# Pairwise interaction tower on one core: look-ups spaced by GpSimd's own memsets in place of waits for TensorE

## The reference

```python
e = jnp.stack([tbl_0[ids[:, 0]], ..., tbl_31[ids[:, 31]]], axis=1)      # 1024 x 32 x 64
p, q = e[:, ROW], e[:, COL]                                             # 496 pairs
kp = jnp.einsum('bpj,ipj->bpi', p, kernel)
z = jnp.sum(kp * q, axis=-1)                                            # 1024 x 496
h = jnp.concatenate([z, dense_ctx], axis=1)
h = jnp.maximum(h @ W_top1 + b_top1, 0.0)                               # 512
h = jnp.maximum(h @ W_top2 + b_top2, 0.0)                               # 256
y = h @ W_top3                                                          # 1
```

## Time and profile before

| | |
|---|---|
| time, three runs | 498.26 us median, 494.0 to 500.97 |
| span of the profiled execution | 412.5 us |
| that execution's time outside its span | not recorded; the median of the runs is 85.8 us above the span |
| TensorE busy | 403.7 us, 98% |
| VectorE busy | 298.6 us, 72% |
| ScalarE busy | 259.1 us, 63% |
| GpSimd busy | 231.6 us, 56% |
| look-ups (indirect DMAs) | 244, 945 ns each on GpSimd |
| TensorE's granted clock, mean | 0.996 |

### The profile page before, as it was taken

How to read it: one execution, slowest core, us unless ns; L and a number is a source line. 1 busy time by engine, 2 the same in 40 slices (tenths; PEclk the granted TensorE clock), 3 DMA queues, 4 the chain that set the end, 5 groups by cost and what they waited for, 6 DMA issues and landing times.

```text
span 412.5 us, 10180 instructions
## 1 busy us (share of the span) xinstructions
PE 403.7 (98%) x3421; PEld 254.4 (62%) x3421; DVE 298.6 (72%) x293; ACT 259.1 (63%) x1874; POOL 231.6 (56%) x251
## 2 busy tenths in 40 slices
PE   7889999999999999999999999999999999999997
PEld 5556656667675766666766665666666566654442
DVE  6776887878788887878979798878879888740000
ACT  6476877667577876764796867719978667002221
POOL 6777777777677757776766777677767200000000
PEclk9998999999999999999999999999999999999999
DMA  6665661131281111211211113111311020000000
GB/s 177 210 200 155 191 221 33 27 77 27 37 219 28 29 19 47 61 28 25 63 42 28 25 25 79 24 27 26 79 25 27 15 51 2 2 2 0 2 0 1
DMA packets 18266, 24.31 MB, mean 59 GB/s; under 512 B 6387, under 2 KB 11767, under 8 KB 17958
## 3 DMA queue, kind: packets, MB, share of 16 engines
q1 hardware_dynamic: 10406, 15.64, 13.0%
q0 software_dynamic: 7808, 8.01, 9.7%
HBM read 19.44 MB, written 0.00 MB: 47 GB/s over the span
## 4 chain that ended last, share of the span: by engine, by line
PE 92%; DMA 3%; POOL 3%; issue 1%; ACT 0%
PE u_ps L690 41%; PE z_ps L724 14%; PE u_ps L711 13%; PE z_ps L730 7%; PE u_ps L771 7%; PE t_ps L644 4%; PE u_ps L791 3%; POOL nat L419 3%; DMA nat<-tbl,ids_sb 2%; PE u_ps L697 2%; DMA ids_sb<-ids 1%; PE t_ps L677 0%; PE u_ps L799 0%; ACT y_sb L571 0%
## 5 line engine op out<-in xcount | busy, mean ns | idle before, releaser
L419 POOL DMA_INDIRECT nat<-tbl,ids_sb x244 | 230.5, 945 | 90.7 <-issue 56.6
L607 DVE TENSOR_TENSOR prod<-u_ps,rows 128x1024 f32<-128x1024 f32 x184 | 213.5, 1218 | 56.7 <-PE u_ps L690 56.7
L504 ACT ACTIVATE pass_prod<-pass_prod 128x64 f32<-128x64 f32 x896 | 214.3, 243 | 22.1 <-DVE pass_prod L618 22.1
L690 PE MATMUL u_ps<-rows,k_sb 64*128 64x256 f32 x1472 | 176.2, 387 | 0.0
L504 ACT ACTIVATION_READ_ACCUMULATOR pass_prod<-pass_prod 128x1 f32 x896 | 169.9, 190 | 0.0
L690 PEld LDWEIGHTS u_ps<-rows,k_sb 64*128 64x128 f32 x1472 | 139.0, 188 | 46.0 <-DVE pass_prod L618 13.4
L618 DVE TENSOR_TENSOR pass_prod<-u_ps,nat 128x1024 f32<-128x1024 f32 x56 | 67.2, 1215 | 1.2 <-PE u_ps L711 1.2
L711 PE MATMUL u_ps<-k_sb,rows 64*128 64x256 f32 x448 | 61.5, 394 | 0.6 <-ACT rows L492 0.6
L724 PE MATMUL z_ps<-prod,sel 128*32 128x512 f32 x512 | 61.6, 598 | 0.0
L492 ACT ACTIVATE rows<-t_ps 128x512 f32<-128x512 f32 (+1 forms) x38 | 19.6, 516 | 54.2 <-PE t_ps L644 54.0
L711 PEld LDWEIGHTS u_ps<-k_sb,rows 64*128 64x128 f32 x448 | 40.6, 186 | 14.6 <-DVE prod L607 9.6
(11 more groups left out here) (50 smaller groups left out, 78.9 us busy)
## 6 DMA issues: line engine op xcount, KB each, us to landing
by_self<-rows SPq DMA_DIRECT2D x32, 128.0 KB
nat<-tbl,ids_sb POOLq DMA_INDIRECT x244
k_sb<-kern SPq DMA_DIRECT2D x3, 768.0 KB, 5.6
k_sb<-kern SPq DMA_DIRECT2D x2, 640.0 KB, 5.7
k_sb<-kern SPq DMA_DIRECT2D x1, 1152.0 KB, 5.2
k_sb<-kern SPq DMA_DIRECT2D x2, 512.0 KB
rows<-w SPq DMA_DIRECT2D x1, 1024.0 KB, 6.6
rows<-tbl SPq DMA_DIRECT2D x4, 224.0 KB
```

The lines of the kernel that those rows point to most:

```text
L419: pool.indirect_dma_start(nat_of(m, n)[:, h * EMBED:(h + 1) * EMBED], None, tables[f], bass.IndirectOffsetOnAxis(ids_sb[:, col:col + 1], 0 ...
L504: op = nc.scalar.activation(of, of, ACT.Copy, accum_out=z_nat[:, b % 2, s, row:row + 1])
L607: nc.vector.tensor_tensor(to, u, by.unsqueeze(1).to_broadcast([P, 2, 2, SIZE]), ALU.mult).then_inc(prod_ready, 1)
L690: op = nc.tensor.matmul(u[:, h, :], k_sb[part, k_of(d), side, :], rows[part, tile, cols_of(b)], start=True, stop=True)
```

## The change

From m = SPACED = 12 on, the two waits ahead of a look-up are left out. In their place GpSimd writes zeros to a tensor `zeros` of 128x128 f32 that nobody reads, and waits for the semaphore of this write, with a count that is higher by one each time; then it issues the look-up. The waits of tiles m < 12, the ring's wait and the wait ahead of tile 0 stay, and so do the order and all work of the other engines.

```diff
+SPACED = 12
...
+        zeros = sb("zeros", [P, P])
...
+        zeros_there = sem("zeros_there")
...
                 for n in range(SUBS):
                     for h in range(2):
-                        _, pieces, quads = PLAN.in_front(m, 2 * n + h)
-                        if pieces:
-                            pool.wait_ge(u_ready, pieces)
-                        if quads:
-                            pool.wait_ge(summed, quads)
+                        if m < SPACED:
+                            _, pieces, quads = PLAN.in_front(m, 2 * n + h)
+                            if pieces:
+                                pool.wait_ge(u_ready, pieces)
+                            if quads:
+                                pool.wait_ge(summed, quads)
+                        else:
+                            nc.gpsimd.memset(zeros[:], 0.0).then_inc(zeros_there, 1)
+                            pool.wait_ge(zeros_there, 4 * (m - SPACED) + 2 * n + h + 1)
                         f = 2 * tile + h
                         col = (b * SUBS + n) * FIELDS + f
                         pool.indirect_dma_start(
```

## The result

The changed kernel takes 594.13 us (median of four runs, 592.71 to 596.87), the kernel before beside it 497.08 us (494.0 to 500.97). The ratio is 1.197, with a 95% interval of [1.1917, 1.2023]. I had forecast 546 us: the sign is right, but the cost is 97 us and not 48.

A forecast was written before the change was run, and what follows sets the result against it. TensorE was taken to bound the kernel, with GpSimd's look-ups hidden; steps of 1.58 us would delay it 47.5 us, so 412.5 + 47.5 = 460, plus 85.8 gives 546 us; range 509 to 598 us.

The forecast's parts named there:

- The sum by late look-ups: TensorE's transposes wait for later look-ups: 47.5 us at pair 58/59, span 412.5 to 460, time 546 us.
- L: The prediction's theory: look-ups come later and TensorE waits for them, delay D = 192p - 255.9 for a step p.
- The step of 1.58 us: GpSimd, look-up start to start from tile 12 on: 0.94 + 0.20 + 0.20 + 0.24 us, ends 1.44 and 1.72.
- the memset must sit out: GpSimd, between a look-up's reported end and the memset's start: 0.20 us taken, between 0.12 and 0.30.
- Rival B: On GpSimd the memset starts at the look-up's reported end: step 1.38 us, delay 9.1, time 507 us; chance 0.12.
- The 2.2 us of landing: Time from a look-up's start until its data has landed, taken alike for all pairs, about 2.2 us.
- Rival D: All 1.25 us of a look-up lie ahead of the memset: step 1.69, 567 us; 0.2 within the forecast's 0.66.
- I leave the 85.8 as it is: The runs' median 498.26 us lies 85.8 above the profiled span; this was added unchanged to the span of 460.
- Nothing on TensorE's path goes with them: gain at the end, nothing: Removing the waits ahead of 208 look-ups, 15 us in all with the ring's, was priced at nothing.
- Last start near 376: Sign on GpSimd: the last look-up would start near 376 us, where the profile before had 322.22.
- Clock: TensorE's low clock, 1.7 us of work per wait, would only eat waiting; after the last wait +1.7 us could show.
- rival C: Changing between memset and look-up makes look-ups last 1.27 us: 628 us, milder forms 573 to 598; chance 0.12 together.

The follow-up runs named there:

- both: The kernel before with its waits kept and the memsets with their waits added from tile 12 on; 439.04 us on chip 7, ratio 1.0629.
- before_third: The kernel before, unchanged, run once more for its profile; 491.17 us beside 492.59, ratio 1.0007.
- waits_off_again: The kernel before with the two waits left out from tile 12 on and no memset in their place; 635.69 us beside 492.59, ratio 1.2973.
- after_again: The changed kernel, unchanged, run again; 577.8 us (564.16 to 578.72), the kernel before beside it 491.12.
- cols360: The changed kernel with a memset of 360 two-byte columns in place of 128 f32 columns; 493.34 us beside 492.59, ratio 1.0046.

## Why the prediction was wrong

**The sum by late look-ups: near on a 412 chip, and worth nothing in the runs that I forecast.** On chip 7 the memsets cost 26.7 us, L with the measured step 21 to 23.5. In the changed kernel all look-ups landed 40 us and more ahead of their transposes, so the 48 us of the forecast aren't among the 97. That the sign came out right is luck. The changed kernel itself never ran on a 412 chip; 433 to 439 us there is my estimate from L and `both`.

**The step of 1.58 us: too large by 0.14.** The term was the 0.20 us that "the memset must sit out". It is 0.00. The 0.30 us between two look-ups belong to the next one's start and not to the last one's end; my split of 0.12 to the end rested on look-ups that wait for other engines. The memset's 0.22 and the round trip's 0.27 were near what I took (0.20, 0.24). Rival B's reasoning was right and its 1.38 too low by these. The 2.2 us of landing were 2.44 at pair 58/59, and 5 beside the load of the weights. Rival D, and with it the rule of the Trainium skill that the instruction goes on past its reported end (Perfetto Trace Analysis, "DMA Instruction — SWDGE (GPSIMD)"), doesn't show here: GpSimd did its memset from that end on.

**"I leave the 85.8 as it is": wrong, and the first failed step.** I took the difference of the runs' median and one execution's span for time outside the span. Time outside is 1.8 us. The 85.8 us lie inside the span, in executions of a kind that the profile didn't show, in which TensorE is held up (`before_third`: span 489.1 us), and such time isn't left as it is by a change to the look-ups.

**"Nothing on TensorE's path goes with them: gain at the end, nothing": wrong, and the step that cost most.** It was true for the profile that I read and false for the runs that I forecast. On 490 chips taking the waits out costs 143 us (waits_off_again), with a memset of 0.22 us in their place still 87 to 97 by the medians (73 in the fastest run of after_again). I had bounded the removal below by nothing without a reason that excludes a loss: I asked who waits for GpSimd, not what its pauses are worth to the others.

**The signs that I named.** Look-ups 1.58 us apart: 1.44. Last start near 376: 472.5. Transposes that wait for look-ups, 18 times and 48 us together: none among the 24 pairs, instead GpSimd waits 106.2 us for the transposes. TensorE's share down to 88%: 81%. Clock: a mean of 0.874, below full in all windows with look-ups; I had hidden it in waits for look-ups, and it did lie beside waits, of another kind. That 594 falls into my range of 509 to 598 is luck: its upper end was rival C's, whose mechanism (look-ups as slow as the first, 1.27 us) isn't there: they last 0.95.

**What stays open.** What makes one chip a 490 chip; and what it is inside such a chip that delays TensorE's instructions and the news of them behind a row of look-ups. Shown is only that the look-ups' spacing sets the size, that in one run plain transfers don't do it, and that it isn't there at once: at the start an update due 9 us into the row was late, beside the tower those up to 15 us into the row were on time. Whether the mean rate or the step within a row counts is open. The look-ups' own data isn't late on these chips: from issue to last packet they take 2.1 us in the median on both kinds. The packets that load instructions take no longer either, medians from 0.96 to 1.12 us on both kinds.

One rival I didn't test: that the recording of the profile itself takes part. All of these times are of executions whose span was recorded. And the traces of 490 chips lack records: of the 3904 semaphore updates that 244 look-ups make, they hold 1023 to 1592 (2339 in `cols360`), those of executions of the 412 kind 3763 to 3871. Beside the tower the 490 chip recorded 91 of 512, the 412 chip all 512; of the 1536 updates of the 96 plain transfers chip 6 recorded all. So updates of look-ups, or their records, are what gets lost or merged there; that fits a jam on the way of these updates as well as a jam in the recording, and no run here tells the two apart.

## What to carry to other kernels

Set the span of the profiled execution against the very time of that execution; where the median of the runs is far above, the profile is of another kind of execution, and the difference isn't overhead. A wait that costs nothing in a profile may be what couples a running-ahead engine to the one that it disturbs: before taking it out, ask how that engine behaves when the other falls behind. If look-ups by GpSimd must be spaced, 1.53 us from start to start did no measurable harm where 1.44 cost 15 to 20%, but the waits did as well, and memsets that space look-ups at 1.44 us cost 27 us on the other chips, so the kernel before stays the best of those tried. And before a delay of transfers is forecast by one pair of tiles, look at what else is being loaded beside each pair.

## What the runs showed of the hardware

The same program takes 412 us on two chips and 486 to 501 on the others. On one of these, beside 32 look-ups in a row at 1.25 us, semaphore updates of finished matmuls arrived up to 22.8 us late, while the records of those matmuls show no gap; in the main loop TensorE was fed one matmul each 0.73 us. On another, 96 plain transfers at 0.5 us each, with over twice the bytes per second (62 GB/s against 27), did neither. On GpSimd a memset starts with the recorded end of an indirect DMA (0.00 us), lasts 0.22 us for 128 columns, 0.31 for 240 and 0.11 for one, and 0.27 us pass to the look-up that waits for it. A look-up takes 2.1 us from issue to its last packet in the median, and 5.0 us were measured beside a load of weights.
